# A causal convolution moved from VectorE into TensorE's input projection, in the front of a Mamba + mixture-of-experts kernel

## The reference, cut to what matters

```
xn = layernorm(x) * ln_w + ln_b                  # 128 channels
xi, z = split(xn @ W_in)                         # 256 + 256 channels
xc[t] = sum_{j=0..3} conv_w[:, j] * xi[t - 3 + j] + conv_b    # causal, per channel
u = silu(xc);   dt_r, B, C = split(u @ W_xproj)  # 8 + 64 + 64
delta = softplus(dt_r @ W_dt + b_dt)
h[t] = exp(delta*A) * h[t-1] + (delta*u)[t] B[t];   y[t] = C[t] . h[t]   # the scan
out = x + ((y + u*D) * silu(z)) @ W_out
```

## Time and profile before

| | us |
|---|---|
| median of 3 runs (lowest, highest) | 2373.51 (2368.64, 2374.96) |
| the profiled execution | 2374.5 |
| its span | 2372.7 |
| busy in the span: PE, DVE, ACT, POOL | 2152.9, 2068.1, 1520.5, 977.3 |
| busy in the span: PE weight load | 1275.1 |

### The profile page before, as it was taken

How to read it: one execution, slowest core, us unless ns; L and a number is a source line. 1 busy time by engine, 2 the same in 40 slices (tenths; PEclk the granted TensorE clock), 3 DMA queues, 4 the chain that set the end, 5 groups by cost and what they waited for, 6 DMA issues and landing times. The chain is left out here.

```text
span 2372.7 us, 49889 instructions
## 1 busy us (share of the span) xinstructions
PE 2152.9 (91%) x16864; PEld 1275.1 (54%) x16864; DVE 2068.1 (87%) x2937; ACT 1520.5 (64%) x1795; POOL 977.3 (41%) x475
## 2 busy tenths in 40 slices
PE   6675999999999999999999965999999999989987
PEld 3331333333333333333333324888899989989876
DVE  7987999999999999999999956777877787787776
ACT  5666888888888888888888841343344334434332
POOL 4325344444434434344343424444444544444342
PEclk7665999999999999999999986999999999999998
DMA  4777212212222122221222231000100020000000
GB/s 114 224 225 222 49 40 49 45 40 44 43 45 46 39 44 44 45 46 38 47 45 42 46 104 52 1 0 0 36 1 0 1 72 1 0 1 6 9 4 18
DMA packets 354411, 114.38 MB, mean 48 GB/s; under 512 B 282968, under 2 KB 345056, under 8 KB 354080
## 3 DMA queue, kind: packets, MB, share of 16 engines
q1 hardware_dynamic: 349584, 110.26, 19.0%
q10 hardware_dynamic: 4752, 3.15, 0.4%
HBM read 67.45 MB, written 45.88 MB: 48 GB/s over the span
## 5 line engine op out<-in xcount | busy, mean ns | idle before, releaser
L1442 DVE TENSOR_TENSOR_SCAN arena<-behind 128x1040 f32<-128x1040 f32 x512 | 1156.9, 2309 | 9.8 <-ACT behind L927 6.2
L997 ACT ACTIVATE arena<-PS,arena 128x512 f32<-128x512 f32 x512 | 348.3, 689 | 544.7 <-PE PS L1210 543.8
L917 ACT ACTIVATE behind<-PS 128x1024 f32<-128x1024 f32 x512 | 526.7, 1029 | 133.8 <-DVE arena L1442 101.1
L1126 PE MATMUL PS<-arena 128*32 128x128 f32 x8192 | 566.1, 406 | 1.8 <-DVE arena L1442 1.8
L927 ACT ACTIVATE behind<-PS 128x1024 f32<-128x1024 f32 x512 | 539.2, 1053 | 7.5 <-PE PS L1109 3.8
L1222 PE MATMUL PS<-arena 128*128 128x128 f32 x4096 | 483.8, 278 | 23.2 <-DVE arena L1591 23.0
L1222 PEld LDWEIGHTS PS<-arena 128*128 128x128 f32 x4096 | 480.5, 195 | 34.4 <-DVE arena L1591 22.7
L715 POOL COPY behind<-carry 128x64 f32<-128x64 f32 x128 | 209.7, 1639 | 514.7 <-DVE arena L1442 374.0
L1210 PE MATMUL PS<-parts_xh,parts_w 128*128 128x512 f32 x1536 | 391.1, 409 | 25.8 <-DVE parts_w L1468 15.3
L1126 PEld LDWEIGHTS PS<-arena 128*32 128x32 f32 x8192 | 235.4, 119 | 290.7 <-issue 212.6
L1109 PE MATMUL PS<-arena 96*128 96x512 bf16 x1024 | 314.9, 390 | 53.8 <-ACT behind L927 35.1
(11 more groups left out here) (120 smaller groups left out, 1451.7 us busy)
## 6 DMA issues: line engine op xcount, KB each, us to landing
dl_d<-arena SPq DMA_DIRECT2D x48, 256.0 KB, 3.5
du_d<-arena SPq DMA_DIRECT2D x48, 256.0 KB, 3.6
arena<-dl_d SPq DMA_DIRECT2D x512, 24.0 KB
arena<-b_d SPq DMA_DIRECT2D x64, 192.0 KB
arena<-du_d SPq DMA_DIRECT2D x512, 24.0 KB
b_d<-arena SPq DMA_DIRECT2D x48, 128.0 KB, 2.9
u_d<-behind SPq DMA_DIRECT2D x8, 512.0 KB, 3.7
sz_d<-arena SPq DMA_DIRECT2D x8, 512.0 KB, 4.7
```

The lines of the kernel that those rows point to most:

```text
L917: nc.scalar.activation(seg(dA[:, half])[:, :, 1:], PS[:, 0:2, :].rearrange("p j (i t) -> p (j i) t", t=TC), ACT.Exp).then_inc(exp_done, 1)
L997: nc.scalar.activation(hT[:, e % 2, c], PS[:, HIDDEN[(GT * e + c) % 3], :], ACT.Gelu, bias=bias1[:, lp, e * GT + c:e * GT + c + 1]).then_i ...
L1126: last = nc.tensor.matmul(PS[32 * j:32 * j + 32, 4 + kk, 0:DB], cd[:, pair, j, 32 * i:32 * i + 32], seg(hb[kk])[:, :, 1 + 16 * j + i], sta ...
L1442: nc.vector.tensor_tensor_scan(hb[kk][:, q * QD * SEG:(q + 1) * QD * SEG], dA[:, q % 2], dB[:, G_, lo:lo + QD * SEG], 0.0, ALU.mult, ALU.a ...
```

## The change

The convolution is linear, so each tap j can be folded into the projection: wtap[j] = W_in[:, 0:256] * conv_w[:, j] along the columns. `inner` becomes four matmuls for each half of the channels, accumulated in PSUM, each against xnT shifted by one column. The three columns of halo now belong to xnT, which is copied by ScalarE (or zeroed) ahead of the take; xi, conv, take_xi, convolve and its pads go. Silu reads PSUM directly, and stands ahead of the Silu of the gate.

On TensorE the convolution of item k + 1 is made in iteration k, its first half ahead of W_dt and its second behind it. Before the loop, the taps are loaded and the four products made on DVE, and TensorE waits for them. The turn of item 1's x stands behind item 0's convolution and gate.

SyncE stores each part when it is done: part 0 ahead of c, parts 1 and 2 behind it.

```diff
+        wtap = take(KC, DI)
+        taps_s = take(KC, DI)
-        xnT = [take(TT) for _ in range(2)]
+        xnT = [take(KC - 1 + TT) for _ in range(2)]
-            def store_parts(k):
+            def store_part(k, w):
                 it, bb = k // 2, k % 2
-                sp.wait_ge(a_p2, k + 1)
-                for p in range(PAIRS):
+                sp.wait_ge((a_p0, a_p1, a_p2)[w], k + 1)
+                for p in [p for p in range(PAIRS) if X_PART[p] == w]:
...
             load_x(0)
+            sp.dma_start(taps_s.rearrange("p t d -> p (t d)"), taps).then_inc(taps_in, 16)
             load_x(1)
...
+                if k > 0:
+                    store_part(k - 1, 0)
                 sp.wait_ge(a_bc, k + 1)
                 sp.dma_start(c_d[it, bb], bc_t[bb][0:N]).then_inc(c_stored[bb], 16)
...
                 if k > 0:
-                    store_parts(k - 1)
+                    store_part(k - 1, 1)
+                    store_part(k - 1, 2)
...
@@ ScalarE, take_xnT
+                    if k // 2 % 2:
+                        nc.scalar.activation(xnT[bb][:, 0:KC - 1], xnT[bb][:, TT:], ACT.Identity).then_inc(a_halo, 1)
+                        act.wait_ge(a_halo, k // 4 * 2 + bb + 1)
+                    else:
+                        nc.scalar.activation(xnT[bb][:, 0:KC - 1], ident_s[:, 0:KC - 1], ACT.Identity, scale=0.0)
+                nc.scalar.activation(xnT[bb][:, KC - 1:], PS[:, 4 * bb, :], ACT.Identity, bias=vecs_s[:, 1:2],
                                      scale=vecs_s[:, 0:1]).then_inc(a_xnT, 1)
@@ ScalarE, iteration k
                 if k > 1:
                     act.wait_ge(a_stored[bb], A_STORES * (k // 2))
+                    act.wait_ge(a_du, k - 1)
+                act.wait_ge(a_xip, HALVES * (k + 1))
+                for h in range(HALVES):
+                    last = nc.scalar.activation(u_s[bb][:, h], PS[:, 4 * bb + h, :], ACT.Silu,
+                                                bias=chan_s[:, h, KC:KC + 1])
+                last.then_inc(a_u, 1)
                 act.wait_ge(a_zp, k + 1)
                 nc.scalar.activation(sz_s[bb], PS[:, 4 * bb + 2:4 * bb + 4, :], ACT.Silu).then_inc(a_sz, 1)
-                act.wait_ge(a_conv, k + 1)
...
-                if 0 < k < LAST:
-                    take_xi(k + 1)
@@ TensorE
-            def inner(k):
+            def inner(k, h):
                 bb = k % 2
-                pe.wait_ge(a_xnT, k + 1)
-                if k > 1:
+                if h == 0:
+                    pe.wait_ge(a_xnT, k + 1)
+                elif k > 1:
                     pe.wait_ge(a_brest, k - 1)
-                for h in range(HALVES):
-                    last = nc.tensor.matmul(PS[:, 4 * bb + h, :], win_s[:, h * P:(h + 1) * P], xnT[bb],
-                                            start=True, stop=True)
+                for t in range(KC):
+                    last = nc.tensor.matmul(PS[:, 4 * bb + h, :], wtap[:, t, h * P:(h + 1) * P],
+                                            xnT[bb][:, t:t + TT], start=(t == 0), stop=(t == KC - 1))
                 last.then_inc(a_xip, 1)
...
-            for k in range(2):
-                turn_x(k)
-                inner(k)
-            gate_of(0)
+            pe.wait_ge(a_pad, 1)
+            pe.wait_ge(a_wtap, KC)
+            turn_x(0)
+            for h in range(HALVES):
+                inner(0, h)
+            gate_of(0)
+            turn_x(1)
...
                 if k > 0:
                     turn_du(k - 1)
+                if k < LAST:
+                    inner(k + 1, 0)
...
                 last.then_inc(a_v, 1)
+                if k < LAST:
+                    inner(k + 1, 1)
...
                 if k < ITEMS - 2:
                     turn_x(k + 2)
-                    inner(k + 2)
@@ DVE
+            for t in range(KC):
+                nc.vector.tensor_tensor(wtap[:, t], win_s[:, 0:DI], taps_s[:, t], ALU.mult).then_inc(a_wtap, 1)
...
             for k in range(ITEMS):
                 bb = k % 2
-                convolve(k)
```

More of the change, by code:

```diff
@@ L42, with build @@
 NG = NT // GT
-def build(nc, x, vecs, chan, a_log, ident, w_in, w_xproj, w_dt, w_out,
+def build(nc, x, vecs, chan, taps, a_log, ident, w_in, w_xproj, w_dt, w_out,
           router_w, router_b, ln_g, ln_b, w1, b1, w2, b2, out):
@@ L169, in build @@
         space[0], limit[0] = arena, ARENA
-        dd, rest, slip, lg, sz_s, conv, part, b_part = ([None, None] for _ in range(8))
+        dd, rest, slip, lg, sz_s, part, b_part = ([None, None] for _ in range(7))
         at_[0] = 0
@@ L200, in build @@
         at_[0] = LOWER + HB
-        xi = [take(HALVES, KC - 1 + TT) for _ in range(2)]
+        xnT = [take(KC - 1 + TT) for _ in range(2)]
         sz_s[1] = take(HALVES, TT)
@@ L204, in build @@
         at_[0] = LOWER + HB + RD
-        conv = [take(HALVES, TT) for _ in range(2)]
+        taps_s = take(KC, DI)
         slip[0] = take(HALVES, TT)
@@ L284, in build @@
         a_btp = sem("a_btp")
-        a_xi = sem("a_xi")
         a_pad = sem("a_pad")
-        a_conv = sem("a_conv")
+        taps_in = sem("taps_in")
+        a_wtap = sem("a_wtap")
+        a_halo = sem("a_halo")
         a_u = sem("a_u")
@@ L310, in build @@
         a_link = sem("a_link")
-        a_tap = sem("a_tap")
         a_rl = sem("a_rl")
@@ L451, in load_x @@
                              .rearrange("(s p) h -> p s h", p=P)).then_inc(a_x[bb], 16)
-            def store_parts(k):
+            def store_part(k, w):
                 it, bb = k // 2, k % 2
-                sp.wait_ge(a_p2, k + 1)
-                for p in range(PAIRS):
-                    src = part[bb][X_PART[p]]
+                sp.wait_ge((a_p0, a_p1, a_p2)[w], k + 1)
+                for p in [p for p in range(PAIRS) if X_PART[p] == w]:
+                    src = part[bb][w]
                     sp.dma_start(dl_d[it, bb, p].rearrange("(h p) t -> p h t", p=P),
@@ L544, in _ @@
                                  b_part[bb][W_PART[p]].rearrange("p k b n -> p k (b n)")).then_inc(a_rows[bb], 16)
-            store_parts(LAST)
+            for w in range(PARTS):
+                store_part(LAST, w)
             for i in range(2):
@@ L618, in _ @@
             for bb in range(2):
-                last = nc.gpsimd.memset(xi[bb][:, :, 0:KC - 1], 0.0)
+                last = nc.gpsimd.memset(xnT[bb][:, 0:KC - 1], 0.0)
             last.then_inc(a_pad, 1)
@@ L870, in _ @@
                 take_xnT(k)
-                take_xi(k)
             for k in range(ITEMS):
@@ L1032, in gate_of @@
                 for h in range(HALVES):
-                    last = nc.tensor.matmul(PS[:, 4 * bb + 2 + h, :], win_s[:, (2 + h) * P:(3 + h) * P], xnT[bb],
+                    last = nc.tensor.matmul(PS[:, 4 * bb + 2 + h, :], win_s[:, (2 + h) * P:(3 + h) * P], xnT[bb][:, KC - 1:],
                                             start=True, stop=True)
@@ L1287, in input_norm @@
                 scaled(lambda s: xt[bb][:, s], mv_a[:, bb], rs_a[:, bb], lambda s: xn[bb][:, s], 4).then_inc(a_xn, 1)
[L1289 to L1313, removed]
             def steps(k):
@@ L1337, in _ @@
                 input_norm(k)
+            dve.wait_ge(weights, WEIGHTS)
+            dve.wait_ge(taps_in, 16)
+            for t in range(KC):
+                nc.vector.tensor_tensor(wtap[:, t], win_s[:, 0:DI], taps_s[:, t], ALU.mult).then_inc(a_wtap, 1)
             dve.wait_ge(a_start, 1)
@@ L1664, in _ @@
             finish(NG - 1, 1)
-_INS = ["x", "vecs", "chan", "a_log", "ident", "w_in", "w_xproj", "w_dt", "w_out",
+_INS = ["x", "vecs", "chan", "taps", "a_log", "ident", "w_in", "w_xproj", "w_dt", "w_out",
         "router_w", "router_b", "ln_g", "ln_b", "w1", "b1", "w2", "b2"]
@@ L1685 @@
                                 halves(L0_attn_b_dt), halves(L0_attn_D)], 2),
+        "taps": np.concatenate([f(L0_attn_conv_w).reshape(DI, KC).T.reshape(1, KC * DI)] * P, 0),
         "a_log": f(L0_attn_A_log),
```

16 lines of the change are left out of this document (removed).

## The result

The changed kernel takes 2367.41 us (median of 20 runs, 2366.08 to 2368.70) where the kernel before took 2372.30 in 20 runs beside it (2368.64 to 2374.96): ratio 0.9981, interval 0.9974 to 0.9987. It is 4.9 us faster, 0.2%, inside the 0.3% that the prediction called no change. The forecast was +10.

The account below looks back on a forecast made before the run. TensorE was to replace VectorE as the bound of the front's step: W_xproj(7) +8.8 us, +1 behind it, total +9.8 on 2374.5 gives 2384.3, less 1.0 for the median: 2383 us. Range holding 8 in 10: 2363 to 2399.

Parts of the forecast that it names:

- The step, 24.5 us: One item's step in the front: 20.7 us of TensorE work plus 3.8 idle, against 23.6 before.
- The hand-over: From TensorE's turn of x through ScalarE's halo copy, take and Silu to the next W_xproj: 3.8 us of idle TensorE.
- rival (b): Clock falls again inside the step, at W_dt or B: 27.3 us in two steps of three, 2400 us; chance 0.13.
- (c): Clock falls only at the gap and rises once W_xproj is through: step 22.6 us, time 2372; chance 0.19.
- TensorE is later by 2 us: Behind W_dt in a step: TensorE needs 9.7 us to end the turn of x, ScalarE 7.7 from Abs to its take.
- DVE is not the bound: In the front's steps VectorE's other work is 12 us a step, so it no longer binds; the opposite got no chance.
- POOL's long subtraction stalls the Ln correction instead: On VectorE in each step: a possible stall, even 3 us of it lying under TensorE; no chance of its own.
- Items 0 and 6: Steps priced apart: item 0 without a turn of delta*u 22.9 us, item 6 without a turn of x 21.6.
- The start, 29.9: Ahead of the steps: tap load, four products and item 0's convolution put W_xproj(0) at 29.9 instead of 22.90, +7.0 us.
- The tail: From W_xproj(7) to the first scan: +1 us, bounds -2 and +3, with part 0 of item 6 stored ahead of c.
- The stores: SyncE's queue: twelve stores take 9.7 us of a step's 24.5 and stay hidden; six move ahead of c.
- The weighed rule: Continuous TensorE work keeps full clock, so the denser front would run at it throughout: step 20.9 us, 2360 us; chance 0.22.

Follow-up runs that it names:

- experiment 1: Changed kernel with both halves of the next item's convolution ahead of W_dt; 2391.04 us, ratio 1.0085.
- experiment 2: Changed kernel with both halves of the next item's convolution behind W_dt; 2363.98 us, ratio 0.997.
- experiment 8: Changed kernel with the first two turns of x ahead of TensorE's wait for the tap products and item 0's convolution; 2357.42 us, ratio 0.994.
- experiment 9: Changed kernel with c of item 7 stored ahead of part 0 of item 6; 2364.26 us, ratio 0.9963.
- experiment 4: Changed kernel with all twelve stores of an item again behind its last part and behind c; 2371.62 us, ratio 0.9996 to the kernel before.
- experiment 11: Changed kernel with TensorE order W_dt, first half, B, second half, turn of x, gate; early first turns of x, c of item 7 first; 2333.75 us.
- experiment 6: Changed kernel with both halves behind W_dt and the turn of x directly behind them, ahead of B and gate; 2374.03 us.
- experiment 5: Changed kernel with the turn of x ahead of the gate and the gate's matmuls issued three times for items 1 to 6; 2359.31 us, ratio 0.9952.

## Why the prediction was wrong

**The step, 24.5 us: failed, measured 21.2.** Its two terms fared differently. The hand-over was right (3.8; measured 3.86, the halo copy 0.19 of it). The pieces were put at 20.7 and took 17.30, and nearly all of the 3.4 is clock:

| piece | predicted | measured |
|---|---|---|
| W_xproj | 3.5 | 3.34 |
| turn of delta*u | 1.6 | 0.87 |
| convolution | 8.1 | 7.08 |
| W_dt | 1.9 | 1.90 |
| B | 2.4 | 1.73 |
| gate | 2.4 | 1.78 |
| turn of x | 0.8 | 0.60 |

In the step of the table the only piece at half clock is the one behind the gap. I had taken B and gate from rows of the kernel before, 2.70 and 2.94, as if such mixed durations belonged to these operations. They belonged to the order around them: two narrow pieces side by side, W_dt and B, as the gate behind such a pair showed again in five of the seven steps of experiment 1. Why it stayed at full clock in the other two is open. The change put a dense half between them. I named that as an argument against rival (b) and did not carry it into the sum. The likeliest case should have been (c), the clock that falls at the gap alone. Its step of 22.6 was still 1.4 too long, and that again in pieces sized from mixed rows: B 0.6, the turn of delta*u 0.5, convolution and W_xproj 0.2 each.

**"TensorE is later by 2 us": failed**, from the same cause. ScalarE's side of it was right, 7.7 from Abs to the halo (144.73 to 152.44). TensorE's 9.7 behind W_dt were 7.65 (144.56 to 152.21). The two tie. Experiments 1 and 2 show it: a half moved ahead of W_dt costs 3.2 us a step, a half moved behind it brings nothing where there is a turn of x.

**DVE is not the bound: right.** It is busy 94.5 us of 148.5. The freed 8 us a step did buy something, against "the freed DVE time buys nothing": the step fell by 2.4, which is what TensorE and ScalarE left.

**POOL's long subtraction stalls the Ln correction instead: right as a mechanism.** That correction averaged 1638 ns over the seven steps where it was 1225 of its own. Timelines of the two engines in the changed kernel:

```profile
150.25 3.81 POOL L678 TENSOR_TENSOR arena<-arena 128x2048 bf16<-128x2048 f32 x1 [12.16 <-ACT arena L868]
```
```profile
152.57 2.57 DVE L1298 TENSOR_TENSOR arena<-arena 128x1024 f32<-128x1024 f32 x1 [1.42 <-ACT arena L903]
```

DVE ends 1.1 behind POOL's 154.06, as if it had begun only then. The Trainium skill, "SBUF — State Buffer", section "Who interferes with whom", says that a DVE instruction with two SBUF inputs contends with a GpSimd instruction that reads SBUF; the trace agrees. It costs nothing in these steps, since the turn of delta*u never waits in them. Behind W_xproj(7) it does cost: the same instruction took 2.82 at 175.07, the turn of delta*u then waited 0.94 for DVE (180.95), and it and W_dt ran at half clock (1.94 and 3.78).

**Items 0 and 6.** Item 6 was put at 21.6 and took 21.60; there the turn of delta*u and a part of the half did run at half clock (1.70 and 3.90 start to start, for the 1.6 and 4.05 taken), which the other steps mostly did not. Item 0 was put at 22.9 and took 20.05, the clock again.

**The start, 29.9: right**, measured 29.21. The four products took 0.35 each (0.45 predicted) and ended at 12.2 as predicted; the convolution of item 0 took 9.07 for 9.7.

**The sum.** W_xproj(7) was put at 196.9 and came at 177.67, 19.2 earlier: 0.7 from the start, 2.9 from item 0, the rest from five steps, 3.1 on average. The tail was put at +1 with bounds of -2 and +3; at the first scan it is +1.9 (27.0 for 25.1). Its mechanism, part 0 ahead of c, is right by experiments 8 and 9 together (2.4 us of waiting with it, none without). In the changed kernel's own profile it can't be told from the clock: of the 1.9, 1.6 is Abs, 9.0 behind W_xproj(7) for 7.4 before, and c was issued 15.9 behind it for 13.7 before. Between the first scan (-8.5) and the end (-7.6) 0.9 is lost, which I did not trace.

**The stores.** The prediction took the queue of SyncE for hidden but for c. At steps of 21 it isn't: with the old stores (experiment 4) the tail is 3.2 us longer, 30.2 for 27.0, and the median 4.2. That the split is worth nothing at the old steps and that much at the new ones is the part of the result that no step of the prediction had.

**The weighed rule.** The rows of after: from 44 to 60 us the clock was 0.89 at 12.32 us of PE busy, and was 0.50 at 14.94 before. Less busy time and a higher clock: the busy share of a stretch did not tell its clock here. The Trainium skill, "TensorE: Matmul & The Clock Gate", section "Why this matters for your kernels", promises the full clock for continuous work; the trace agrees for the dense stretch from the turn of delta*u to the turn of x (1.00 from 138.25 to 152.21), and experiment 11 (granted clock 0.99 from W_xproj(0) to W_xproj(7)) for a whole front. It does not agree for the kernel before, where TensorE worked without a gap for 13.62 us at half clock, and there the measurement decides. The window, with the columns of the earlier trace rows:

```profile
46.56:60.18 13.62, 13.62 (x36) 8.18 (x36) 11.07 (x14) 9.05 (x9) 4.29 (x2) 0.50 0.04 10
```

## What to carry to other kernels

Where TensorE's clock changes inside a step, don't price a piece by its row in the old order; price it at the clock that its new neighbours keep, and price each gap with the half-clock time of what follows it (here 1.6 us behind one of 3.9, and 5 behind one of 2.6). Close every loop of a step separately and compare them: a piece is free on the one that does not hold it, and of two loops that tie, shortening one brings nothing. Two edits that are each worth nothing can be worth something together when one makes late what the other brings forward.

## What the runs showed of the hardware

- An fp32 multiplication of only 8 rows (W_dt) ran at full clock between dense pieces (1.98 us in all seven steps of the changed kernel). Behind a gap of 2.58 us and a turn in experiment 6 it took 3.78, at half clock, and the convolution behind it began at half as well.
- The length of the gap alone does not decide. W_xproj ran at half clock behind 3.87 us of idle in the changed kernel, but at full (1.94) behind 3.69 in experiment 8 and behind 3.39 in experiments 5 and 9. Behind 1.96 it lost some once in experiment 11 (the row at 110.99), and nothing behind the same 1.96 at 40.51. PE of experiment 8, its second W_xproj:

```profile
40.88 1.94 PE L1060 MATMUL PS<-behind 128*72 128x512 f32 x4 [3.69 <-ACT behind L879]
```
